# Windowed attention on eight cores: pairing score banks, dealing projections by thirds, splitting the output step

## The reference

```python
h = shift_token(x)                 # second half of the columns comes from the row before
q, k, v = split(h @ wqkv, 3)       # 8 heads of 64: 3 x 512 columns
q = l2norm(q) * qs;  k = l2norm(k) * ksc
q, k = rotary_xpos(q, k)
o = local_attention(q, k, v)       # WINDOW = 512
x = x + o @ wo
h = layernorm(shift_token(x)) * lg + lb
a, g = split(h @ w1 + b1, 2)
x = x + (a * gelu(g)) @ w2 + b2
```

## Time and profile before

| | |
|---|---|
| median of three runs | 3925.93 us (3921.85 to 3931.12) |
| the profiled execution | 3913.0 us, span of its slowest core 3911.4 us |
| spans of the eight cores | 3874.4 to 3911.4 us |
| mean granted clock | 0.945 to 0.950 |
| busy, slowest core: PE, DVE, ACT, POOL | 3388.4, 1403.7, 884.7, 1091.7 us |
| DMA in the span | 386.59 MB, 99 GB/s |

### The profile page before, as it was taken

The page is one execution under the profiler, slowest core; times in us unless marked ns, Lnnn a source line. Parts: engine busy times, 40 slices in busy tenths (PEclk is TensorE's granted clock), DMA queues, the critical chain, the costliest instruction groups (busy, mean ns, idle before and its releaser), DMA issues.

```text
span 3911.4 us, 55703 instructions; the slowest of 8 cores (3874.4 to 3911.4 us)
## 1 busy us (share of the span) xinstructions
PE 3388.4 (87%) x20890; PEld 1662.8 (43%) x20890; DVE 1403.7 (36%) x2537; ACT 884.7 (23%) x1328; POOL 1091.7 (28%) x993
## 2 busy tenths in 40 slices
PE   6888857888874998889999968888859999999998
PEld 3444423444442443344444534444424444444445
DVE  2455544454542222222222224555432322222221
ACT  1211113444440111101111114445411111111111
POOL 4344425553311112212111024343212222122211
PEclk9999978999997999999999988999979999999999
DMA  9433334893326143443111141433271112222112
GB/s 159 127 140 135 141 120 78 131 159 111 108 105 218 49 86 79 104 109 80 47 54 60 44 126 28 119 87 115 92 240 70 68 62 87 81 73 73 65 44 76
DMA packets 149112, 386.59 MB, mean 99 GB/s; under 512 B 14324, under 2 KB 49394, under 8 KB 147826
## 3 DMA queue, kind: packets, MB, share of 16 engines
q1 hardware_dynamic: 96578, 279.74, 20.0%
q0 software_dynamic: 38768, 70.27, 12.8%
q10 hardware_dynamic: 13504, 33.03, 2.5%
HBM read 342.10 MB, written 153.62 MB: 127 GB/s over the span
## 4 chain that ended last, share of the span: by engine, by line
PE 70%; DVE 9%; DMA 8%; issue 4%; POOL 4%; ACT 3%; ACTq 2%; SPq 0%; DVEq 0%; POOLq 0%
PE m_pu L61 30%; PE m_pd L61 15%; PE a_pr L61 9%; PE p_yp L61 4%; PE a_sc L61 3%; PE p_qp L61 3%; PE a_tb L61 2%; DVE a_t L61 2%; POOL a_qn L61 2%; ACTq L61 2%; DMA m_xa<-xasp 2%; PE a_av L61 2%; ACT a_pT L61 1%; DMA m_xr<-xasp 1%; DMA swo<-fwo 1%
## 5 line engine op out<-in xcount | busy, mean ns | idle before, releaser
L61 PE MATMUL m_pu<-wA,m_w1b 128*128 128x512 bf16 (+2 forms) x4752 | 995.1, 370 | 0.0
L61 PEld LDWEIGHTS m_pu<-wA,m_w1b 128*128 128x128 bf16 x4752 | 462.6, 98 | 505.2
L61 ACT ACTIVATE wA<-m_pu,m_b1c 128x512 bf16<-128x512 f32 (+3 forms) x396 | 264.7, 669 | 1721.4 <-PE m_pu L61 1599.0
L61 PE MATMUL a_pr<-wA,a_xT 128*128 128x512 bf16 x1776 | 465.9, 398 | 55.3 <-DVE a_t L61 43.5
L61 PE MATMUL m_pd<-m_w,m_h 128*128 128x512 bf16 x2208 | 503.6, 379 | 0.0
L61 ACT ACTIVATE a_pT<-a_sc,a_nb 128x1024 bf16<-128x1024 f32 (+1 forms) x344 | 375.0, 1103 | 341.1 <-PE a_sc L61 339.2
L61 DVE SCALAR_TENSOR_TENSOR m_h<-m_pu,m_b1c,wA 128x512 bf16<-128x512 f32 (+2 forms) x288 | 208.4, 728 | 621.9 <-ACT wA L61 621.9
L61 POOL TENSOR_TENSOR m_xr<-m_xr,m_b2r 128x1024 f32<-128x1024 f32 x69 | 161.7, 2347 | 840.3 <-DMA m_xr<-xasp 491.0
L61 PE MATMUL m_pu<-wA,w1a 128*128 128x512 bf16 (+2 forms) x1440 | 320.4, 384 | 74.4 <-DVE m_h L61 72.8
L61 PEld LDWEIGHTS m_pd<-m_w,m_h 128*128 128x128 bf16 x2208 | 213.1, 98 | 243.6
L61 POOL TENSOR_TENSOR m_rs<-m_rs,mhalf 128x1 f32<-128x1 f32 x69 | 39.3, 570 | 943.0 <-DVE m_rs L61 943.0
(11 more groups left out here) (100 smaller groups left out, 3310.6 us busy)
## 6 DMA issues: line engine op xcount, KB each, us to landing
p_x<-xin SPq DMA_DIRECT2D x39, 512.0 KB, 5.8
xfsp<-p_xf SPq DMA_DIRECT2D x39, 512.0 KB, 2.8
a_xr<-xfsp SPq DMA_DIRECT2D x35, 512.0 KB, 6.3
xasp<-a_xr SPq DMA_DIRECT2D x35, 512.0 KB, 3.2
m_xr<-xasp SPq DMA_DIRECT2D x35, 512.0 KB, 4.9
xlsp<-m_xr SPq DMA_DIRECT2D x35, 512.0 KB, 3.4
a_xr<-xlsp SPq DMA_DIRECT2D x35, 512.0 KB, 5.8
xbsp<-a_xr SPq DMA_DIRECT2D x35, 512.0 KB, 3.5
```

Source lines behind the costliest of these rows:

```text
L61: ins = getattr(h, meth)(*args, **kw)
```

## The change

**Scores.** The body of a bank is split into `bank` (the two heads' score products) and `edge` (masks and exponential). The (hp, u) pairs of a group are put in one list and taken two at a time: bank, bank, edge, edge, then one yield of 1300. The buffer is now SC[(hp * banks + u) % 2]. Before a pair that holds the last bank of a hp, the waiting value products are emptied; after one that doesn't, n or 2n steps of them are taken.

**Projections.** `step_q(j, s)` is one third of the old step. The sum of squares and POOL's work on it follow the second third (s == 1), not the third one.

**Output.** `step_p` is split: `step_o` has the four transposes and the copy, `step_p` the products, the sum and the store.

**The list in side.** It now goes, for block i: third 0, step_n of the block before, step_x of the next block, third 1, step_o, third 2, step_p, step_r of the block before. A last turn (i = number of blocks) has step_n, step_o, step_x of the next group's first block, step_p and step_r. The stated costs go from 6980 and 2640 to 6200 and 2000 a block; the conversions still come one to an element of the list. After the weave of the last group, `side(NG, NG - 1)` replaces the plain loop over step_p.

```diff
@@ -678,61 +678,61 @@
-        def step_q(j):
+        def step_q(j, s):
...
-            v1, s_ = [], []
-            for s in range(3):
-                Z = next_pr()
...
-                    if kc == 3:
-                        yield 870
-                if s < 2:
-                    h = s * 512
-                    s_.append(op("scalar", "activation", s2.t[:, h:h + 512], Z.t[:, :], AF.Square,
-                                 need=[t] + s2.free))
...
-                    Z.free = [v1[-1]]
+            Z = next_pr()
+            need = Z.free + [T.full, t_wq]
...
+                if kc == 3:
+                    yield 870
+            if s < 2:
+                h = s * 512
+                q = op("scalar", "activation", s2.t[:, h:h + 512], Z.t[:, :], AF.Square, need=[t] + s2.free)
+                s2.full = (s2.full if s else []) + [q]
+                v = op("vector", "tensor_tensor", sap(a.t, h, [[64, 8], [1, 64]]),
+                       sap(Z.t, 0, [[64, 8], [1, 64]]),
+                       sap(tm.t, s * 128, [[0, 8], [1, 64]]), ALU.mult, need=[q, tm.full] + a.free)
+                w = op("vector", "tensor_tensor", sap(c2.t, h, [[64, 8], [32, 2], [1, 32]]),
+                       sap(Z.t, 32, [[64, 8], [-32, 2], [1, 32]]),
+                       sap(tm.t, s * 128 + 64, [[0, 8], [1, 64]]), ALU.mult, need=c2.free)
+                a.full = (a.full if s else []) + [v, w]
+                Z.free = [w]
+                if s == 1:
+                    tm.free = [w]
+                    m.sums = op("vector", "tensor_reduce", m.t[:, 0:16], sap(s2.t, 0, [[64, 16], [1, 64]]),
+                                AX.X, ALU.add, need=s2.full + m.free)
+                    s2.free = [m.sums]
+                    m.sums = op("gpsimd", "tensor_scalar", m.t[:, 0:16], m.t[:, 0:16], 1e-24, None, ALU.max,
+                                need=[m.sums])
+                    a.full = op("gpsimd", "tensor_tensor", a.t[:], a.t[:], c2.t[:], ALU.add, need=a.full)
+                    c2.free = [a.full]
+            else:
...
+                Z.free = [e]
+                V.full = (V.full if i else []) + [e] + kept
+                T.free = [t]
+            yield 870
...
@@ -830,54 +830,71 @@
...
-            for hp in range(4):
+
+            def bank(hp, u):
+
+                tl = banks[u]
+                S = SC[(hp * len(banks) + u) % 2]
...
+                edges = any(kb >= 0 or kb + 4 < n for kb, _, _, _ in tl)
+                for kb, lo, w, col in tl:
+                    K = kT[(g + (kb // 4)) % 3]
+                    for h in range(2):
+                        t = self.pe(S.t[:, h * 512 + col * 128:h * 512 + (col + w) * 128],
+                                    pap(K.t, 64 * h, 64, hp * 512 + (kb % 4) * 128, [[1, 128]]),
+                                    pap(Q.t, 64 * h, 64, hp * 512 + lo * 128, [[1, w * 128]]),
+                                    kb == tl[0][0], not edges and kb == tl[-1][0], need=need,
+                                    sig=not edges and kb == tl[-1][0] and h == 1,
+                                    tile_position=(64 * h, 0))
+                        need = ()
+                return S, wide, edges, t
+
+            def edge(hp, u, S, wide, edges, t):
+
+                tl = banks[u]
...
+                for h in range(2):
+                    for c, s, k in runs:
+                        t = self.pe(S.t[:, h * 512 + c * 128:h * 512 + (c + k) * 128], self.ident[:],
+                                    mul[:, s * 128:(s + k) * 128], False, c == runs[-1][0], need=[t_ml],
+                                    sig=h == 1 and c == runs[-1][0])
                 P = pT[hp % 2]
...
-                for u, tl in enumerate(banks):
-                    S = SC[u % 2]
-                    wide = max(col + w for _, _, w, col in tl) * 128
...
-                    e = op("scalar", "activation", sap(P.t, u * 1024, [[512, 2], [1, wide]]),
-                           sap(S.t, 0, [[512, 2], [1, wide]]), AF.Exp, bias=nb[:, 4:5], scale=8.0,
-                           need=[t, n3] + P.free)
-                    S.free = [e]
+                e = op("scalar", "activation", sap(P.t, u * 1024, [[512, 2], [1, wide]]),
+                       sap(S.t, 0, [[512, 2], [1, wide]]), AF.Exp, bias=nb[:, 4:5], scale=8.0,
+                       need=[t, n3] + (P.free if u == 0 else []))
+                S.free = [e]
+                return e, t
+
+            todo = [(hp, u) for hp in range(4) for u in range(len(banks))]
+            toks = []
+            for k in range(0, len(todo), 2):
+                burst = todo[k:k + 2]
+                if any(u == len(banks) - 1 for _, u in burst):
+
+                    for c in state["back"]:
+                        yield c
+                done = [(hp, u) + bank(hp, u) for hp, u in burst]
+                for d in done:
+                    e, t = edge(*d)
                     toks.append(e)
-                    yield 650
-                    for _ in range(n if u in (0, 2) or n < 4 else 0):
-                        c = next(state["back"], None)
-                        if c is not None:
-                            yield c
-                P.free = []
-                for c in state["back"]:
-                    yield c
-                if hp == 0:
-                    ot[g % 2].full = []
-                state["back"] = av(g, hp, P, place, toks)
+                    if d[1] == len(banks) - 1:
+                        if d[0] == 0:
+                            ot[g % 2].full = []
+                        state["back"] = av(g, d[0], pT[d[0] % 2], place, toks)
+                        toks = []
+                yield 650 * len(burst)
+                if not any(u == len(banks) - 1 for _, u in burst):
+                    ends = any(u == len(banks) - 1 for _, u in todo[k + 2:k + 4])
+                    for c in itertools.islice(state["back"], 2 * n if ends else n):
+                        yield c
             Q.free = [t]
             kT[(g - 1) % 3].free = [t]
@@ -887,10 +904,10 @@
...
-        def step_p(g, i):
+        def step_o(g, i):
 
             j = groups[g][i]
-            O, b, oo = ot[g % 2], xres[j % 4], oT[j % 2]
+            O, oo = ot[g % 2], oT[j % 2]
...
-            e = op("vector", "tensor_copy", oo.t[:], TB.t[:, 0:512], need=[t] + oo.free)
-            TB.free = [e]
-            yield 900
+            oo.full = op("vector", "tensor_copy", oo.t[:], TB.t[:, 0:512], need=[t] + oo.free)
+            TB.free = [oo.full]
+            yield 250
+
+        def step_p(g, i):
+
+            j = groups[g][i]
+            b, oo = xres[j % 4], oT[j % 2]
             ev = []
             for nh in range(2):
                 Z = next_pr()
-                need = Z.free + [e, t_wo]
+                need = Z.free + [oo.full, t_wo]
...
@@ -922,29 +944,32 @@
...
             seq = []
-            ps_ = [step_p(gp, i) for i in range(np_)]
-            for i in range(len(qs)):
-                if i == 0:
-                    seq.append(step_x(qs[0]))
-                if i + 1 < len(qs):
-                    seq.append(step_x(qs[i + 1]))
-                seq.append(step_q(qs[i]))
-                if i > 0:
+            for i in range(max(len(qs), np_) + 1):
+                q = i < len(qs)
+                p = 1 <= i <= np_
+                if q:
+                    seq.append(step_q(qs[i], 0))
+                    if i > 0:
+                        seq.append(step_n(qs[i - 1]))
+                    if i + 1 < len(qs):
+                        seq.append(step_x(qs[i + 1]))
+                    seq.append(step_q(qs[i], 1))
+                elif i > 0 and i == len(qs):
                     seq.append(step_n(qs[i - 1]))
-                if i > 1:
-                    seq.append(step_r(qs[i - 2]))
-            seq += ps_[0:1]
-            if qs:
-                seq.append(step_n(qs[-1]))
-            if len(qs) > 1:
-                seq.append(step_r(qs[-2]))
-            seq += ps_[1:3]
-            if qs:
-                seq.append(step_r(qs[-1]))
-            seq += ps_[3:]
+                if p:
+                    seq.append(step_o(gp, i - 1))
+                if q:
+                    seq.append(step_q(qs[i], 2))
+                elif i == len(qs) and gq + 1 < NG:
+                    seq.append(step_x(groups[gq + 1][0]))
+                if p:
+                    seq.append(step_p(gp, i - 1))
+                if 1 <= i <= len(qs):
+                    seq.append(step_r(qs[i - 1]))
...
@@ -958,6 +983,8 @@
...
         load(first + 1)
+        for _ in step_x(groups[first][0]):
+            pass
         for g in range(first, ga + 1):
             for _ in side(g, -1):
                 pass
@@ -972,17 +999,16 @@
...
-            s_cost = (len(groups[g + 1]) * 6980 if g + 1 < NG else 0) + (
-                len(groups[g - 1]) * 2640 if g > ga else 0)
+            s_cost = (len(groups[g + 1]) * 6200 if g + 1 < NG else 0) + (
+                len(groups[g - 1]) * 2000 if g > ga else 0)
```

(5 more changed lines are left out.)

## The result

The changed kernel took 3902.38 us (median of six executions) against 3923.82 us for the kernel before on the same chip: ratio 0.9949, interval 0.9936 to 0.9961, 20 us less. One of the six took 4296 us with one die at a lower granted clock; such executions, before and in all experiments, are left out of the ratios, and rows are taken from a die that they did not touch. The forecast was 3891 us in a range of 3808 to 3944, and most likely "faster".

A forecast was written before the change was run, and what follows sets the result against it. TensorE's work and waits (busy 87% of the span) were taken as the bound. First attention -9 us and second -26 made -35: 3913.0 to 3878, plus 12.9 for the median, 3891 us; range 3808 to 3944.

The forecast's parts named there:

- Part 1: Attention scores: pairing banks saves 0.2 us a pair, 17.6 and 16.8 us, against 0.8 us of waits a group.
- Part 2: Attention side work: 5.9 us of waits go, 6.4 come with Part 1's 0.8: nothing, between -6 and +3 a group.
- the waits really vanish: Rival: woven work covers DVE's chain, no 6.4 us of new waits in twelve groups, -77 us more, 3815 us; chance 0.22.
- new waits outweigh: Rival: ACT's doubled bursts and DVE's queue cost 3 us a group more, +36, 3927 us; chance 0.12.
- Part 3: Attention groups: side work lasts to 87% of a group, not 80%; with the clock, 0.5 us a group less.
- Part 4: Run-up before each attention's scores: earlier step_n removes most of PE's wait through POOL, -9 us first, -6 second.
- Part 5: First attention: group 5's x load queues behind all 54 conversions, lands at 827; PE waits some 21 us.
- the signs that were to show the forecast right: Half-row entries halved, output-copy waits over 1 us, one long x wait, second attention 20 to 30 us shorter, groups 57 to 60.

The follow-up runs named there:

- the longer yield: The changed kernel with the last step of the first head's value products yielding 440 and not 180: ratio 0.9898 to the kernel before, -40 us.
- The run with both repairs: The changed kernel with scores one bank at a time and 20 conversions a group as before the change: ratio 0.9773 to the kernel before, -89 us.
- a slower pace: New order, unpaired scores, output copy ahead of the reduction, with weight conversions after 16 steps a group and not 20: ratio 0.9679 to the kernel before, -126 us.

## Why the prediction was right in total and wrong in its parts

**Part 1, pairing: the step that failed.** Its saving was sized well. In one full group at clock 1.00, PE by tile and shape, the score and mask products of before (the group of 59.1 us in the earlier trace rows) are busy for 16.2 us and those of the changed kernel for 14.6 us. A group's length without its waits says the same: it is 48.5 us in the changed kernel (clock 1.00) and 50.2 in the new order with unpaired scores (clock 0.996). So ten pairs save 1.6 to 1.7 us, where 2.0 was taken. Most of it is in the masks, 5.5 us before. Of the changed kernel:

```profile
L61 PE MATMUL a_sc<-a_mul,ident 128*128 128x128 bf16 x48 | 4.4, 221 | 0.0
L61 PE MATMUL a_sc<-a_qT,a_kT 64*128 64x512 bf16 x16 | 3.0, 381 | 1.8 <-ACT a_pT L61 1.8
L61 PE MATMUL a_sc<-a_qT,a_kT 64*128 64x384 bf16 x16 | 2.3, 325 | 0.0
```

What failed is the sentence "Without Squares ahead of them in ACT's queue that just fits; I take 0.8 us a group, between 0 and 3". It asks what stands ahead of the exponentials and not what stands behind them. A second exponential holds a Square behind it by up to its own length, 1.1 us, and the rotations, the reduction, the output copy, the projection bank and PE hang on that Square in a row. Pairing also gathers the value products into batches, which the single value bank can't take. Together that is 4.5 to 4.9 us a group, where 0.8 us was taken, and on the new order some 12 us in the second attention's group of three banks (52.1 us for 40.5, means over the cores). Forecast: 28 us less for the gaps (11.6 + 16.8), of which 0.8 us in each of twelve groups come back. Measured: 63 us more alone, 44 more on the new order. That the pair's second half feeds the waits for the output copy and a_t is shown by spreading it. That pairing causes the waits for the value bank is shown by the run without it (5.3 us over the whole kernel, for 50.1). That it does so by the batches is shown in the group of three banks by the longer yield and only argued elsewhere.

**Part 2, the new order.** The waits for the transpose bank's copies to a_kT and a_xT went as forecast. The wait for the output copy came where it was forecast, behind the reduction, at 1.7 us each and two a group (3.4 us) against 1.3 us and three (3.9). But a good part of it belongs to pairing: without pairing it is 0.5 us each. "Nothing, between -6 and +3 us a group" had its likeliest value wrong for the order by itself: its waits fall from 8.3 to 5.7 us a group, and full groups from 60.5 to 56.8 us. The rival "the waits really vanish" describes the new order, and "new waits outweigh" describes pairing. Two errors of opposite sign met in the sum.

**Part 3, the clock.** The direction is as forecast: over the six full groups of the second attention the mean clock rose from 0.973 to 0.987. Its price can be read from the changed kernel's own groups, 58.8 us at 1.00 and 60.4 at 0.97 with the same 10.3 us of waits. By that the rise is worth an estimated 0.8 us a group, where 0.5 was taken. It is most of the 1.0 us by which the mean full group is shorter. At a clock of 1.00 a group is only 0.3 us shorter, since 2 us more of waits eat most of what the order and pairing save in PE's work. What raised the clock stays open.

**Part 4, the run-up.** Right in sign, -15 us for -9 in the first attention; in the second -5 for -6 (47.8 us before, 42.7 after). Which of its waits was sized too small in the first stays open.

**Part 5, the backlog.** The mechanism and the place were right; counted from the entry into the stage (core 7) the landing was 2 us later than forecast and PE came 8 us earlier, so the wait was 31 to 36 us and not 21. The mis-sized term is the gain of the run-up and the first two groups. It costs 34 us of the total by the run that removes it. So the faster order did work in the first attention too, and this ate it.

**By the sum:** the new order gains 98 us without the backlog (64 with it, and its 34), the backlog takes 34 and pairing 44: 20 us are left. (The run with both repairs showed 89 for the 98, with 12.7 us of the wait for x still in it.) The forecast was 35, from a gain on pairing that is a loss, a small gain on the order, and a smaller backlog. The time was in the range by luck: errors of opposite sign cancelled. Of the signs that were to show the forecast right, the long wait for x, the waits for the output copy and groups of 57 to 60 us came; a second attention 20 to 30 us shorter did not, it is 13 us with its run-up.

## What to carry to other kernels

- When work is batched on one engine to save its gaps, price what the batch does to the queue of the engine that takes it over: what stands behind it there, and who waits for that. Here 1.7 us saved cost 4.5 to 4.9 us.
- A list that also paces something else (here one conversion for each element) must not be made finer without looking at that. A transfer queued behind a backlog lands when the backlog lets it, and takes back all that was gained ahead of it.
- Where a change has two halves, forecast and measure each alone: a sum that comes out can hide a half that should be left out. The new order without pairing, with the output copy first and a slower pace, takes 126 us off and not 20.

## What the hardware showed

- Behind the 36 us without work PE came back at half clock. Windows of the changed kernel, from the landing on:

```profile
821.30:826.30 5.00, 4.75 (x25) 2.76 (x27) 1.82 (x3) 0.00 (x0) 0.00 (x0) 0.50 1.08 132
826.30:828.30 2.00, 1.11 (x21) 0.99 (x18) 1.46 (x5) 0.00 (x0) 0.00 (x0) 0.84 1.18 165
828.30:830.30 2.00, 1.79 (x34) 1.27 (x34) 0.53 (x3) 0.06 (x1) 0.00 (x0) 1.00 1.11 187
```

The granted clock was 0.50 (1.2 GHz) for the first 5 us and a third of the next two, and the eight transposes took 1.01 us where they take 0.61 at full clock. A stall that long costs more than its length: by these rows an estimated 2.8 us, half of those 5.6.

- A denser stream of conversions filled the DMA engines earlier: the DMA share was 0.96, 1.03 and 1.01 in three successive groups, where it had been 0.74, 0.83 and 1.00. The queue's end moved forward by the idle time that had been there, as the forecast had counted: from the entry into the stage to the landing it was 275.5 us, for 273.4 forecast (core 7).
